# Edge loops written out over eight steps, and two finishing phases of a four-layer graph network by fifths

## The reference

```python
edge_index = jnp.stack([src, dst])
h = jnp.maximum(_layernorm(x, axis=-1), 0.0)
x = x + _L0_gnn_ref(h, edge_attr_64, ..., src, dst)
h = jnp.maximum(_layernorm(x, axis=-1), 0.0)
x = x + _L1_gnn_ref(h, edge_index, 12500, L1_gnn_W, L1_gnn_b)
h = jnp.maximum(_layernorm(x, axis=-1), 0.0)
x = x + _L2_gnn_ref(h, L2_gnn_W, L2_gnn_c, edge_index)
```

## Time and profile before

| what | value |
|---|---|
| three runs: median (lowest, highest) | 12883.76 us (12857.01, 12890.77) |
| the profiled execution, its own time | 12841.23 us |
| its span, from the first to the last instruction | 12839.5 us |
| mean clock of TensorE granted in it | 0.613 |
| busy share of PE, DVE, ACT, POOL | 52%, 54%, 33%, 58% |

### The profile page before, as it was taken

The page is one execution under the profiler, slowest core; times in us unless marked ns, Lnnn a source line. Parts: engine busy times, 40 slices in busy tenths (PEclk is TensorE's granted clock), DMA queues, the critical chain, the costliest instruction groups (busy, mean ns, idle before and its releaser), DMA issues. The chain is left out here.

```text
span 12839.5 us, 129455 instructions
## 1 busy us (share of the span) xinstructions
PE 6663.3 (52%) x28159; PEld 5268.1 (41%) x28159; DVE 6988.1 (54%) x14158; ACT 4188.1 (33%) x8422; POOL 7478.3 (58%) x7574
## 2 busy tenths in 40 slices
PE   0555555533155555541266666666648454555552
PEld 0333333322155555441266666666643333333331
DVE  4555555555355555521555555555542566666665
ACT  0222222211055555540144444444433222222221
POOL 5666666661666666655055555555546665656665
PEclk9666666665577777775555555555555556666655
DMA  4333333340322222220133333333334333333332
GB/s 88 109 107 109 109 108 109 109 86 30 125 55 55 56 56 56 54 49 10 36 78 78 79 78 78 78 78 77 78 60 98 93 103 102 105 101 107 104 103 78
DMA packets 1317881, 1050.64 MB, mean 82 GB/s; under 512 B 817585, under 2 KB 1034504, under 8 KB 1317034
## 3 DMA queue, kind: packets, MB, share of 16 engines
q0 software_dynamic: 243008, 318.86, 13.5%
q1 hardware_dynamic: 677254, 367.08, 11.2%
q10 hardware_dynamic: 397397, 362.35, 8.5%
HBM read 577.78 MB, written 469.43 MB: 82 GB/s over the span
## 5 line engine op out<-in xcount | busy, mean ns | idle before, releaser
L1165 POOL DMA_INDIRECT h_rows_d<-table,h_idx_d x1840 | 1752.4, 952 | 1393.4 <-PE h_ps_sum L1186 809.5
L633 POOL DMA_INDIRECT rows<-table3s,idx_all x1664 | 1612.5, 969 | 1051.4 <-issue 474.7
L633 POOL DMA_INDIRECT rows<-table,idx_all x1664 | 1712.5, 1029 | 817.0 <-issue 475.0
L940 POOL DMA_INDIRECT m_rows<-table,idx_all x1664 | 1574.0, 946 | 909.2 <-issue 452.8
L970 PE MATMUL m_ps_sort<-m_hot_high,m_hot_low 128*128 128x224 f32 x3328 | 1051.4, 495 | 974.1 <-issue 810.1
L970 PEld LDWEIGHTS m_ps_sort<-m_hot_high,m_hot_low 128*128 128x128 f32 x3328 | 916.0, 281 | 1080.7 <-issue 932.0
L1186 PE MATMUL h_ps_sum<-h_rows_d,h_hot 128*128 128x65 f32 x3680 | 829.5, 416 | 644.6 <-DVE h_rows_d L1323 361.3
L1186 PEld LDWEIGHTS h_ps_sum<-h_rows_d,h_hot 128*128 128x128 f32 x3680 | 793.0, 327 | 728.9 <-issue 728.9
L1204 PE MATMUL h_ps_src<-h_near,h_hot_t 128*128 128x65 f32 x3680 | 838.2, 419 | 457.5 <-DMA h_near<-table 245.4
L780 PE MATMUL ps_out<-ident,sums 128*128 128x128 f32 x3328 | 733.0, 387 | 638.6 <-issue 283.4
L1204 PEld LDWEIGHTS h_ps_src<-h_near,h_hot_t 128*128 128x128 f32 x3680 | 803.0, 330 | 490.4 <-issue 489.5
(11 more groups left out here) (424 smaller groups left out, 14325.4 us busy)
## 6 DMA issues: line engine op xcount, KB each, us to landing
scan<-out_e ACTq DMA_DIRECT2D x832, 256.0 KB
h_near<-table SPq DMA_DIRECT2D x1840, 32.5 KB
run_g<-h_run ACTq DMA_DIRECT2D x230, 260.0 KB
part_b<-part SPq DMA_DIRECT2D x832, 64.0 KB
max_b<-top ACTq DMA_DIRECT2D x416, 128.0 KB
scan<-m_out_e SPq DMA_DIRECT2D x416, 128.0 KB
attr<-in_edge_attr SPq DMA_DIRECT2D x415, 128.0 KB
h_rows_d<-table,h_idx_d POOLq DMA_INDIRECT x1840
```

Source lines behind the costliest of these rows:

```text
L633: pool.indirect_dma_start(out=rows[:, b, k, h * GW:(h + 1) * GW], out_offset=None, in_=table3s.rearrange("n (q f) -> (n q) f", f=HEADS) if ...
L940: pool.indirect_dma_start(out=rows[:, b, k, h * D:(h + 1) * D], out_offset=None, in_=table1, in_offset=bass.IndirectOffsetOnAxis(ap=idx_al ...
L1165: pool.indirect_dma_start(out=rows_d[:, b, k, :], out_offset=None, in_=table2, in_offset=bass.IndirectOffsetOnAxis(ap=idx_d[:, c * BT + k: ...
```

## The change

Three edits. In `steps()` a turn is two rounds of the four buffers, eight steps; each step still uses buffer `c % SLOTS`. A softmax stage then has 25 turns and not 50, the hyperbolic one 27 for most engines and not 55 (SP 28 and not 56). The turn of DVE in the hyperbolic stage grows from 204 to 397 instructions, of SP from 145 to 285, of ACT from 66 to 126, of PE from 126 to 247; in the first softmax stage DVE's grows from 65 to 124 and SP's from 41 to 77. In `finish_softmax` the groups no longer cross a fifth (15 groups of 8, 8, 4 blocks), the layernorm and the store go by fifths, and ACT's relus stand two fifths ahead of the roots. In `finish_mean` PE does `lin1` of the next fifth before `lin2` of this one, DVE computes the next aggregate and keeps the fifth before behind its layernorm, and ACT's copies of both are put between its roots and tanhs.

```diff
--- before.py
+++ after.py
@@ -495,6 +495,7 @@
 
 
 
+            turn = 2 * SLOTS
             deep = -(-(max(lag for lag, _ in stages) + SLOTS) // SLOTS) * SLOTS
 
             def peeled(those):
@@ -504,13 +505,13 @@
                             stage(s - lag, (s - lag) % SLOTS, (s - lag) // SLOTS)
 
             peeled(range(deep))
-            turns = (n - deep) // SLOTS
+            turns = (n - deep) // turn
             with eng.Fori(0, turns) as i:
-                for j in range(SLOTS):
+                for j in range(turn):
                     for lag, stage in stages:
                         c = deep + j - lag
-                        stage(i * SLOTS + c, c % SLOTS, i + c // SLOTS)
-            peeled(range(deep + turns * SLOTS, n + deep))
+                        stage(i * turn + c, c % SLOTS, i * 2 + c // SLOTS)
+            peeled(range(deep + turns * turn, n + deep))
 
         def slot_free(eng, sem, c, each=1, ago=2):
 
@@ -1489,7 +1490,8 @@
                 def ring(g):
                     return slice(g % DEEP * COLS, (g % DEEP + 1) * COLS)
                 ZG = 8
-                zgroups = [(z, min(z + ZG, NB)) for z in range(0, NB, ZG)]
+                zgroups = [(z, min(z + ZG, (q + 1) * FIFTH)) for q in range(FIFTHS) for z in range(q * FIFTH, (q + 1) * FIFTH, ZG)]
+                PER_FIFTH = len(zgroups) // FIFTHS
                 with nc.Block() as block:
                     @block.sync
                     def _(sp):
@@ -1505,9 +1507,10 @@
                         sp.dma_start(final_g.rearrange("(b n) -> n b", n=P), final_i[:, :],
                                      allow_slow_non_contiguous=True).then_inc(put_map, 16)
                         sp.wait_ge(put_map, 48)
-                        sp.wait_ge(normed, 1)
-                        sp.dma_start(nodes(table1), Hn[:, :, :]).then_inc(put, 16)
-                        sp.wait_ge(put, 16)
+                        for q in range(FIFTHS):
+                            sp.wait_ge(normed, q + 1)
+                            sp.dma_start(nodes(table1)[:, fifth(q), :], Hn[:, fifth(q), :]).then_inc(put, 16)
+                        sp.wait_ge(put, 16 * FIFTHS)
 
                     @block.gpsimd
                     def _(pool):
@@ -1630,9 +1633,11 @@
                             v.tensor_tensor(X[:, z0:z1, :], X[:, z0:z1, :],
                                             ps_z[:, g % 2, 0:(z1 - z0) * D].rearrange("p (b f) -> p b f", f=D), ALU.add) \
                                 .then_inc(z_taken, 1)
-                        dve.wait_ge(z_taken, len(zgroups))
-                        layernorm_relu(dve, step, small, X, Hn, var_ready, std_ready)
-                        dve.sem_inc(normed, 1)
+                            q, rest = divmod(g + 1, PER_FIFTH)
+                            if rest == 0:
+                                dve.wait_ge(z_taken, g + 1)
+                                layernorm_relu(dve, step, small, X, Hn, var_ready, std_ready, q, fifth(q - 1))
+                                dve.sem_inc(normed, 1)
 
                     @block.tensor
                     def _(pe):
@@ -1692,10 +1697,12 @@
                         act.wait_ge(var_done, 3)
                         a.activation(cols[:, 4:5], cols[:, 4:5], ACT.Sqrt, bias=cols[:, 7:8], scale=1.0 / N).then_inc(std_out, 1)
                         act.wait_ge(scaled, 1)
-                        for z0, z1 in zgroups:
-                            a.activation(Y[:, z0 * NP:z1 * NP], Y[:, z0 * NP:z1 * NP], ACT.Relu, bias=cols[:, 6:7],
-                                         scale=cols[:, 5:6]).then_inc(relued, 1)
-                        layernorm_std(act, small, eps5[:, :], var_ready, std_ready)
+                        for q in range(FIFTHS + 2):
+                            for z0, z1 in zgroups[q * PER_FIFTH:(q + 1) * PER_FIFTH]:
+                                a.activation(Y[:, z0 * NP:z1 * NP], Y[:, z0 * NP:z1 * NP], ACT.Relu, bias=cols[:, 6:7],
+                                             scale=cols[:, 5:6]).then_inc(relued, 1)
+                            if q >= 2:
+                                layernorm_std(act, small, eps5[:, :], var_ready, std_ready, q - 1, fifth(q - 2))
 
         def atanh_over(dve, step, sem_in, sem_out, k, y, norm, s, out_f, at=slice(0, NB)):
 
@@ -1788,11 +1795,13 @@
                         pe.wait_ge(got_w, 64)
                         nc.tensor.transpose(ps_w, w_rows[:, :], ident[0:D, 0:D]).then_inc(w_turned, 1)
                         pe.wait_ge(w_moved, 1)
-                        for q in range(FIFTHS):
-                            pe.wait_ge(agg_ready, q + 1)
-                            lin1.pe(pe, G, w_t[:, :], q * EACH, (q + 1) * EACH, RING)
-                            pe.wait_ge(p_ready, q + 1)
-                            lin2.pe(pe, G[:, :, 0:D], w_p[:, :], q * EACH, (q + 1) * EACH, RING)
+                        for q in range(FIFTHS + 1):
+                            if q < FIFTHS:
+                                pe.wait_ge(agg_ready, q + 1)
+                                lin1.pe(pe, G, w_t[:, :], q * EACH, (q + 1) * EACH, RING)
+                            if q:
+                                pe.wait_ge(p_ready, q)
+                                lin2.pe(pe, G[:, :, 0:D], w_p[:, :], (q - 1) * EACH, q * EACH, RING)
 
                     @block.scalar
                     def _(act):
@@ -1809,16 +1818,25 @@
                         def tanhs(k, to, of):
                             act.wait_ge(ask_tanh, k)
                             a.activation(to, of, ACT.Tanh).then_inc(tanhed, 1)
+                        lin1.act(act, 0, EACH)
                         for q in range(FIFTHS):
-                            at = fifth(q)
-                            lin1.act(act, q * EACH, (q + 1) * EACH)
+                            at, more = fifth(q), q + 1 < FIFTHS
+                            if q:
+                                lin2.act(act, (q - 1) * EACH, q * EACH - 1)
                             layernorm_std(act, s, eps5[:, :], var_ready, std_ready, q + 1, at)
+                            if q:
+                                lin2.act(act, q * EACH - 1, q * EACH)
                             roots(2 * q + 1, nf[:, at])
+                            if more:
+                                lin1.act(act, (q + 1) * EACH, (q + 1) * EACH + 2)
                             tanhs(q + 1, th[:, at], nf[:, at])
+                            if more:
+                                lin1.act(act, (q + 1) * EACH + 2, (q + 1) * EACH + 3)
                             roots(2 * q + 2, np_[:, at])
-                            if q == FIFTHS - 1:
-                                logarithms(act, ask_log, logged, 1, s)
-                            lin2.act(act, q * EACH, (q + 1) * EACH)
+                            if more:
+                                lin1.act(act, (q + 1) * EACH + 3, (q + 2) * EACH)
+                        logarithms(act, ask_log, logged, 1, s)
+                        lin2.act(act, (FIFTHS - 1) * EACH, FIFTHS * EACH)
                         for h, at in enumerate(halves):
                             roots(2 * FIFTHS + 2 * h + 1, tn[:, at])
                             tanhs(FIFTHS + h + 1, th[:, at], tmp[:, at])
@@ -1842,19 +1860,25 @@
                                 table[:, g * GROUP:(g + 1) * GROUP, 0:D], y[:, 0, 0:GROUP * D].rearrange("p (b f) -> p b f", f=D)),
                                 q * EACH, (q + 1) * EACH)
 
-                        for q in range(FIFTHS):
+                        def aggregate(q):
                             at, here = fifth(q), fifth(q % 2)
                             step(v.tensor_copy(G[:, here, D:2 * D], Hn[:, at, :]))
                             dve.wait_ge(gathered[q], 16 * FIFTH)
                             step(v.tensor_tensor(G[:, here, 0:D], table[:, at, 0:D], bcs(k1[:, at], at), ALU.mult))
                             dve.sem_inc(agg_ready, 1)
-                            if q:
-                                keep(q - 1)
+
+                        aggregate(0)
+                        for q in range(FIFTHS):
+                            at, here = fifth(q), fifth(q % 2)
                             lin1.take(dve, lambda g, y: v.tensor_tensor(
                                 X[:, g * GROUP:(g + 1) * GROUP, :], X[:, g * GROUP:(g + 1) * GROUP, :],
                                 y[:, 0, 0:GROUP * D].rearrange("p (b f) -> p b f", f=D), ALU.add), q * EACH, (q + 1) * EACH)
                             dve.wait_ge(lin1.taken, (q + 1) * EACH)
                             layernorm_relu(dve, step, s, X, Hn, var_ready, std_ready, q + 1, at)
+                            if q:
+                                keep(q - 1)
+                            if q + 1 < FIFTHS:
+                                aggregate(q + 1)
 
                             p = G[:, here, 0:D]
                             step(v.tensor_scalar(p, Hn[:, at, :], EPS2, None, ALU.add))
```

## The result

The changed kernel takes 12,773.6 us in the median of four runs (12,747.9 to 12,780.6), the kernel before 12,880.9 (12,857.0 to 12,890.8). The ratio is 0.9912 with a 95% interval from 0.9896 to 0.9928: 107 us less, clear of noise. I had forecast 12,770.

What follows compares the result with a forecast made beforehand. No engine was taken to be near its limit; waits in each stage bound the kernel. 33 + 24 + 17 + 20 + 17 = 111 us off 12,883.8 gave 12,773, rounded to 12,770, range 12,690 to 12,890.

Steps and rivals of the forecast that it cites:

- the loops' 54 us: Edge loops: back-edge once in eight steps, not four; 17 first softmax, 20 hyperbolic, 17 last softmax, nothing for the mean loop.
- two of its own signs: Profile signs: first softmax gap of 16.37 us once in eight steps, otherwise 15.70; hyperbolic loop under ten fetches in 2000 us.
- finish_softmax: Finishing phase by fifths, products overlapping layernorms: fifths 12.5 us apart, 33 us less, bounds 26 and 38.
- finish_mean: Finishing phase with lin1 of the next fifth ahead: steady fifths 43.7 us against 50.7, 24 us less, bounds 5 and 45.
- The first softmax loop: First softmax edge stage: 25 fewer back-edges at 0.67 us, 17 us less, bounds 0 and 35.
- 25 x 0.67 = 17, that is direct: First softmax loop: a back-edge priced as the difference of two scan gaps, of which one holds it; 17 us.
- The hyperbolic loop: Hyperbolic edge stage: 28 fewer back-edges at 0.7 us, 20 us less, bounds 1.5 and 39.
- only SyncE's back-edge counts: Edge loops: the savings were priced from SyncE's back-edges alone, at 0.67 to 0.7 us each.
- The last softmax loop: Last softmax edge stage: 25 fewer back-edges at 0.7 us, 17 us less, bounds 1 and 35.
- The reload: Rival, 10%: hyperbolic loop's longer body fetched again each turn, 4 x 1.28 x 27 = 139 us more, time 12,932.

Runs made afterwards that it cites:

- dve_short: The changed kernel with DVE's turn in the hyperbolic loop back at four steps; ratio 0.9917 to the kernel before, that stage 3137 us.
- loops_only: The kernel before with only the turns of eight steps, both finishing phases as before; ratio 0.9954, 59 us less.
- the fourth set: Last four runs, all variants of the changed kernel, on another chip; the kernel before took 10,375 us there, the four ratios were 0.9941 to 0.9948.
- hyp_only: The changed kernel with turns of eight steps in the hyperbolic stage alone, four in the other loops; ratio 0.9945 to the kernel before.

## Why the prediction was right, and where it wasn't

**The total** was right: 12,770 against 12,773.6, 111 us less forecast and 107 measured. That it is so near is partly luck. The two phases hold by their mechanism. Of the loops' 54 us (17 + 20 + 17) the profiles show 0, 41 and 16: two wrong terms that cancel. By two of its own signs the part on the loops was wrong: the long gap of the first softmax loop comes as often as before where its rhythm can be read, and the hyperbolic loop has 100 fetches in 2000 us and not under ten.

**finish_softmax** was right in mechanism: 33 us, and 33.2 measured (400.4 to 367.2) in the first pair of profiles. The first fifth comes out to the hundredth (9.15 us from the first product to the layernorm). A fifth takes 12.75 and not 12.5, the store with the start of the next stage 7.9 and not 7, so that from the first product to the next stage 31.1 us are gained; the other 2 lie ahead of the products, where the kernel before moves as much from one profile to the next (400.4 and 398.0).

**finish_mean** was right in mechanism: only two groups are ready after the chain, three still come one by one. The three steady fifths take 41.7, 42.7 and 42.7, not 43.7, which gives 25 and not 21. The first interval got 12.6 us shorter (144.0 to 131.4) where I had 12, and behind the last layernorm 8.3 are lost where I had 9. The first layernorm starts 1.4 us later in the phase. The phase gained 28, not 24.

**The first softmax loop**: the step that failed is "25 x 0.67 = 17, that is direct". The stage gained nothing in six of seven profiles (2558.9 to 2564.6 with turns of eight on any engine, 2560.2 to 2562.9 with four), and in one it lost 17. SyncE's wait of 566 us was the reason at hand, and I let the difference of two gaps outweigh it. The rows of the changed kernel show why that difference was no price. L684 there:

```profile
1096.56 1.27 DVE L684 TENSOR_TENSOR_SCAN top<-part_b,top,ps_score 128x512 f32<-128x512 bf16 x1
...
1104.85 1.27 DVE L684 TENSOR_TENSOR_SCAN top<-part_b,top,ps_score 128x512 f32<-128x512 bf16 x1
...
1120.65 1.27 DVE L684 TENSOR_TENSOR_SCAN top<-part_b,top,ps_score 128x512 f32<-128x512 bf16 x1
...
1128.70 1.27 DVE L684 TENSOR_TENSOR_SCAN top<-part_b,top,ps_score 128x512 f32<-128x512 bf16 x1
...
1145.12 1.27 DVE L684 TENSOR_TENSOR_SCAN top<-part_b,top,ps_score 128x512 f32<-128x512 bf16 x1
```

and SyncE's back-edges in 1060 to 1200, first and last start:

```profile
L509 SPq ALU_OP  x2: 700/714/728, 1086.0 to 1183.3; - x2
L509 SPq FUSED_REGOPS  x2: 3/3/3, 1087.5 to 1184.7; - x2
```

The gap from 1128.70 to 1145.12 is 16.42 us long and there is no back-edge in it: the two in this stretch are at 1086 and 1183. In **dve_short**, whose steps keep this rhythm through the stage, the medians of the eight gaps of a turn are 8.05, 15.82, 8.04, 16.26, 8.05, 15.80, 8.04 and 16.29 us: the longest gap comes twice in a turn, and the one back-edge lies in a gap of 8.04. The longer of two pairs belongs to the four buffers' round, and not to the loop. The difference of two neighbouring gaps coincided with the branch, and I took it for its price.

**The hyperbolic loop**: 20 us forecast. Four profiles with turns of eight on all engines give 3118 to 3154, mean 3134; the three with four 3169 to 3183, mean 3175: 41 us. The price itself held: from the start of SyncE's back-edge to its next instruction it is 42 to 44 us in 56 turns with turns of four, 0.75 each, and 17 to 22 in 28 in those four profiles. The step that failed is that only SyncE's back-edge counts; PE's, ACT's and DVE's together bring about as much as SyncE's (13 each alone, by one profile), and both together three times that. Why the sum is more than its parts I can't show; the scatter of single profiles (37 us) is larger than the parts.

**The last softmax loop**: 17 forecast; 2718 in the mean of three against 2702 in the mean of four, 16, with a scatter of 37 among the three. Right as far as it can be seen.

**The reload**, my slow rival, had a true mechanism and a wrong effect. It happens: 139 packets more, 2.8 us at the branch shown, 76 us in sum. I had priced a turn at 5.1 us by ScalarE's table load; it is 2.8, since only one block is waited for. Packets of that queue start at 7416.7, 7419.9, 7425.5, 7459.6 and 7496.8 in the turn shown, and DVE goes on at 7418.6, behind the first. But the rival needed DVE to be on the path, and **dve_short** shows that it isn't: without the reload the time is the same. By the Trainium skill, "Runtime: NRT & Kernel Launch", "Instruction fetch mechanics", a taken branch out of the window of loaded pages makes the engine wait for a fetch; the trace agrees, with 2.8 us. Its capacity for most engines, 512 instructions, isn't what a body may have in these runs: 397 on DVE and 365 on SyncE were fetched in every turn, and 349 on SyncE were in one kernel and weren't in five others. Whether its blocks of 256 instructions explain it, by where a body lies on them, no run here shows.

**Not forecast at all** is that the loops' part depends on the conditions of the run. Where SyncE's instructions take up to 1.4 us it was 59 us in **loops_only**; in the fourth set nothing of it can be seen. There the fixed price from the Trainium skill, "Advanced Engine Details and Errata", "Control Flow Timing" (about 108 ns for a compare-and-branch), is near: 45 ns for the compare-and-branch itself and 137 for the three instructions of the back-edge in the first softmax stage. An estimate from that, 78 x 0.137, is 11 us in sum, and the runs show no gain. What makes the difference between the sets no run here shows.

## What to carry to other kernels

A chain that runs over the whole width can be cut where its work is already in pieces, and the gain can be worked out to a few microseconds from the rows of one piece: what is ready when the engine comes (here as many groups as there are product buffers) and what still comes one by one. Two neighbouring gaps that differ don't price the one event that lies in the longer; look for the same gap without the event. And a longer loop body trades back-edges for reloads: look at the instruction queue's packets by stage, then ask whether the engine that stands is one that is waited for. Last, a gain on sequencers that one set of runs shows can be absent in the next.

## What the runs showed of the hardware

- A loop body of 397 instructions (DVE) was fetched again in each turn in every kernel that had it, at two places 82 instructions apart among them, with about five packets a turn and 2.8 to 2.9 us at the branch. Bodies of 204 (DVE) and 375 (TensorE, with another queue, q8) weren't. SyncE's body of 349 was fetched again in hyp_only (3.5 us a turn) and in no other kernel that had it; its body of 365 was (3.2 us).
- The same program, the kernel before, took 12,881, 12,817, 12,844 and 10,375 us in four sets of runs. Its profiles and those of its changed forms show the same granted clock (0.61 to 0.62) and nearly the same busy times in all four (TensorE 6593 to 6775 us, GpSimd 7434 to 7495). In the first three, register moves of SyncE's sequencer took up to 1.4 us, and DVE's adds in `finish_mean` waited up to 34 us while GpSimd issued indirect DMAs, one of them for a product that TensorE had ended 20 us before (5985 and 6005.7 in the changed kernel); in the fourth the moves took 0.04 us at most, and those adds waited 4 us at most.
- Two profiles of one program differ by up to 37 us in one edge stage and by up to 5 in a finishing phase.
